# Own semaphores for the weight loads of a mixture-of-experts layer, and two of the loads emitted later

## The chip, the cores and the metric

The kernel runs on the 8 NeuronCores of one Trainium2 chip. The cores do not exchange data: each computes one of the 8 sequences of the batch. What counts is the device time of the slowest core, in microseconds (us).

Each core has a matrix engine (TensorE, PE in the profile; PEld are its weight loads), a vector engine (VectorE, DVE), an activation engine (ScalarE, ACT), a general one (GpSimd, POOL) and SyncE (SP). Each runs its own stream of instructions in order, and they wait for one another on semaphores. DMAs are issued from SyncE's and GpSimd's streams here. Line numbers such as L868 are those of the kernel before.

## The reference

A transformer layer with layer norm ahead of each part. Cut to the second part, in which the change lies:

```python
x = x + attention(layernorm(x))
# flat: [T, D] of layernorm(x); T = 2048 tokens per core, D = 1024, H = 2048, E = 8, top 2
router_probs = softmax(flat @ router_w + router_b)
weights = top-2 of router_probs, zero elsewhere                    # [T, E]
shared_out = gelu(flat @ sw1 + sb1) @ sw2 + sb2
h1 = gelu(einsum('td,edh->teh', flat, rw1) + rb1)                  # all 8 experts, all tokens
expert_out = einsum('teh,ehd->ted', h1, rw2) + rb2
x = x + shared_out + einsum('ted,te->td', expert_out, weights)
```

## The kernel before

The program is written as a plan: `P.emit(engine, fn, waits, inc)` appends one instruction to the list of an engine, with the semaphores and counts that it waits for and the semaphore that it raises. Five semaphores exist: ST, SV and SS, raised by TensorE, VectorE and ScalarE, SQ by the DMAs of SyncE and GQ by the DMAs of GpSimd. `emit` treats the last two in a special way:

```python
        waits = tuple((s, self.cnt[s] if s in ("SQ", "GQ") else v)
                      for (s, v) in waits)
```

A wait for SQ or GQ is thus turned into a wait for all DMAs of that queue that were emitted so far, whichever count was given.

The stages of a core, one behind the other: layer norm and attention with its output projection (to about 1714 us of the profile), second layer norm and router (to about 1846 us), nine experts (to about 4245 us: expert 0 is the shared one, 1 to 8 the routed ones, each over all 2048 tokens), and the store of XRES.

The activations are kept transposed, features on the partitions: XLN (bf16) is the normalised input, XRES (float32) the running result. An expert has W1 (1024 x 2048) and W2 (2048 x 1024), each 4 MB as bf16 in one buffer of its own; the float32 source is cast by the DMA. `emit_mm1(e, tt)` computes a token tile of 512: for each of 16 blocks of hidden features 8 matmuls into one of four slots of PM1 (L729), then a Gelu with the bias B1C by ScalarE into H1G (L746), and for the routed experts a product with WB, the routing weights broadcast to all partitions, by VectorE (L795). `emit_mm2(e, tt)` does for each of 8 output blocks 16 matmuls from H1G and W2 (L817) and one for the bias row B2S (L827) into PM2, and VectorE adds the result to XRES (L834). H1G has two halves, so the order of an expert is mm1(0), mm1(1), mm2(0), mm1(2), mm2(1), mm1(3), mm2(2), mm2(3).

At the head of each routed expert (L843 to L883) five DMAs are emitted on GpSimd, in the order W1 (L845; waits for the last mm1 of the expert before), WROW (L848; one row of routing weights), B1C (L853), B2S (L858) and W2 (L863; the last two wait for the last mm2 of the expert before). Behind them the broadcast is emitted: four times a matmul of ONES with a quarter of WROW into a slot of PM1 (L868) and a copy into WB by VectorE (L877). L868 waits for GQ, for its slot, and for the counts of ScalarE and VectorE as they stand at that point of the plan. Then comes emit_mm1(e, 0).

`barrier()` makes all engines wait for all semaphores; it stands behind the first layer norm, behind attention and ahead of the store.

Of the kernel before, what the change touches and what calls it, by code (L numbers as in the profile page):

```python
# [14 lines left out]
D = 1024  # L15
# [53 lines left out]
def build_program():  # L69
    nc = bass.Bass("TRN2", target_bir_lowering=False)  # L70
# [10 lines left out]
    w2cat = dt("w2cat", [NEXP, 128, (DFF // 128) * D], F32, kind="ExternalInput").ap()  # L81
    b1col = dt("b1col", [NEXP, 128, 16], F32, kind="ExternalInput").ap()
    b2row = dt("b2row", [NEXP, 1, D], F32, kind="ExternalInput").ap()
# [8 lines left out]
    with ExitStack() as ctx:  # L92
        E = ctx.enter_context
# [3 lines left out]
            "SS": E(nc.semaphore("SS")),  # L97
            "SQ": E(nc.semaphore("SQ")),
            "GQ": E(nc.semaphore("GQ")),
        }  # L100
        P = Plan(sems)
        C = P.cnt
# [18 lines left out]
        def barrier():  # L121
            for eng in ("tensor", "vector", "scalar"):
                assert P.tail_inc[eng], f"barrier: {eng} tail lacks inc"
            w = [(k, C[k]) for k in ("ST", "SV", "SS", "SQ", "GQ")]
            for eng in ENGS:
                P.emit(eng, lambda e: e.nop(), waits=w, neutral=True)

        sq_x = []
        for c in range(NCH):
# [3 lines left out]
                inc="SQ", inc_n=16))  # L133
        sq_ones = P.emit("sync", lambda e: e.dma_start(out=ONES[:], in_=c_ones),
                         inc="SQ", inc_n=16)
# [111 lines left out]
        try:  # L247
# [6 lines left out]
            with ExitStack() as actx:  # L254
# [54 lines left out]
                for h in range(min(H, DBG["nheads"])):  # L309
# [32 lines left out]
                    for mt in (range(NMT) if DBG["qkv_parts"] in ("all", "v") else []):  # L342
# [10 lines left out]
                               waits=w)  # L353
# [159 lines left out]
            with ExitStack() as fctx:  # L513
# [12 lines left out]
                gq_rbr = P.emit("gpsimd", lambda e: e.dma_start(out=RBR[:], in_=rwb_row),  # L526
                                inc="GQ", inc_n=16)
                gq_w1 = [P.emit("gpsimd", lambda e: e.dma_start(out=W1[:], in_=w1cat[0]),
                                inc="GQ", inc_n=16)]
                gq_w2 = [P.emit("gpsimd", lambda e: e.dma_start(out=W2[:], in_=w2cat[0]),  # L530
                                inc="GQ", inc_n=16)]
                gq_b1 = [P.emit("gpsimd",
                                lambda e: e.dma_start(out=B1C[:, 0:16], in_=b1col[0]),
                                inc="GQ", inc_n=16)]
                gq_b2 = [P.emit("gpsimd",
                                lambda e: e.dma_start(out=B2S[0:1, 0:D], in_=b2row[0]),
                                inc="GQ", inc_n=16)]

                ln2_done = emit_ln([[] for _ in range(NCH)])
                _ckpt("ln2")  # L540
# [171 lines left out]
                def emit_mm1(e_i, tt, wb_ready, mm1_first_w):  # L712
                    buf = tt % 2
                    last_marker = None
                    for ht in range(16):
# [20 lines left out]
                            if r is not None:  # L736
                                tmm = r
                        h1sl = H1G[:, buf * 8192 + ht * 512: buf * 8192 + (ht + 1) * 512]
                        gw = [("ST", tmm), ("GQ", gq_b1[e_i])]
                        if ht == 0:  # L740
                            gw.append(h1g_free[buf])
                        if e_i == 0 and tt == 0 and ht == 0:
# [58 lines left out]
                def emit_mm2(e_i, tt, h1_ready):  # L801
                    buf = tt % 2
                    last_st = 0
                    for dtl in range(NCH):
                        slot = state["rot2"] % 4
                        state["rot2"] += 1
                        psv = PM2[:, slot * 512:(slot + 1) * 512]
                        for kc in range(16):
                            w = []
                            if kc == 0:  # L810
                                w = [pm2_free[slot], h1_ready]
                                if len(vx_hist) >= 2:
                                    w.append(("SV", vx_hist[-2]))
                                if dtl == 0 and tt == 0:
                                    w.append(("GQ", gq_w2[e_i]))
                            P.emit("tensor",
                                   lambda e, psv=psv, kc=kc, dtl=dtl, buf=buf: e.matmul(  # L817
                                       psv,
                                       W2[:, kc * D + dtl * 128: kc * D + (dtl + 1) * 128],
                                       H1G[:, buf * 8192 + kc * 512:  # L820
                                           buf * 8192 + (kc + 1) * 512],
                                       start=(kc == 0), stop=False),
                                   waits=w)
                        rhs = (WB[0:1, tt * 512:(tt + 1) * 512] if e_i > 0
                               else ONES[0:1, 0:512])
                        tr = P.emit("tensor",
                               lambda e, psv=psv, dtl=dtl, e_i=e_i, rhs=rhs: e.matmul(  # L827
                                   psv,
                                   B2S[0:1, dtl * 128:(dtl + 1) * 128],
                                   rhs, start=False, stop=True),  # L830
                               waits=[("GQ", gq_b2[e_i])], inc="ST")
                        last_st = tr
                        vx = P.emit("vector",
                               lambda e, psv=psv, dtl=dtl, tt=tt: e.tensor_add(  # L834
                                   xres(dtl)[:, tt * 512:(tt + 1) * 512],
                                   xres(dtl)[:, tt * 512:(tt + 1) * 512], psv),
                               waits=[("ST", tr)], inc="SV")
                        pm2_free[slot] = ("SV", vx)
                        state["xadd"] = vx
                    return ("ST", last_st)  # L840

                for e_i in range(min(NEXP, DBG["nexp"])):
                    if e_i > 0:  # L843
                        gq_w1.append(P.emit("gpsimd",
                                lambda e, e_i=e_i: e.dma_start(out=W1[:], in_=w1cat[e_i]),  # L845
                                waits=[w1_free], inc="GQ", inc_n=16))
                        gq_wrow = P.emit("gpsimd",
                                lambda e, e_i=e_i: e.dma_start(  # L848
                                    out=WROW[:], in_=WSB[e_i - 1:e_i, :]),
                                waits=[("SV", router_done_sv), wrow_free],  # L850
                                inc="GQ", inc_n=16)
                        gq_b1.append(P.emit("gpsimd",
                                lambda e, e_i=e_i: e.dma_start(  # L853
                                    out=B1C[:, (e_i % 2) * 16:(e_i % 2) * 16 + 16],
                                    in_=b1col[e_i]),
                                waits=[b1_free[e_i % 2]], inc="GQ", inc_n=16))
                        gq_b2.append(P.emit("gpsimd",
                                lambda e, e_i=e_i: e.dma_start(  # L858
                                    out=B2S[0:1, 0:D],
                                    in_=b2row[e_i]),  # L860
                                waits=[b2_free], inc="GQ", inc_n=16))
                        gq_w2.append(P.emit("gpsimd",
                                lambda e, e_i=e_i: e.dma_start(out=W2[:], in_=w2cat[e_i]),  # L863
                                waits=[w2_free], inc="GQ", inc_n=16))
                        wb_evac = 0
                        for r in range(4):
                            tb_ = P.emit("tensor",
                                    lambda e, r=r: e.matmul(  # L868
                                        PM1[:, r * 512:(r + 1) * 512],
                                        ONES[0:1, 0:128],  # L870
                                        WROW[0:1, r * 512:(r + 1) * 512],
                                        start=True, stop=True),
                                    waits=[("GQ", gq_wrow), pm1_free[r],
                                           ("SS", C["SS"]), ("SV", C["SV"])],
                                    inc="ST")
                            wb_evac = P.emit("vector",
                                    lambda e, r=r: e.tensor_copy(  # L877
                                        WB[:, r * 512:(r + 1) * 512],
                                        PM1[:, r * 512:(r + 1) * 512]),
                                    waits=[("ST", tb_), wb_free], inc="SV")  # L880
                            pm1_free[r] = ("SV", wb_evac)
                        wrow_free = ("ST", tb_)
                        wb_ready = ("SV", wb_evac)  # L883
                    else:
                        wb_ready = ("SV", 0)

                    mm1_first_w = [("GQ", gq_w1[e_i])]
                    if e_i == 0:
                        mm1_first_w += [("SV", ln2_done),
                                        ("SV", router_done_sv),  # L890
# [2 lines left out]

                    h1_ready = {}
                    h1_ready[0] = emit_mm1(e_i, 0, wb_ready, mm1_first_w)
                    if DBG["stop"] == "mm1" and e_i == 0:
                        h1_ready[1] = emit_mm1(e_i, 1, wb_ready, mm1_first_w)
                        _DBGREF["H1G"] = H1G
                        _ckpt("mm1")
# [193 lines left out]
```

How the kernel before makes its waits and increments, by code:

```python
        def run(e, _w=waits, _f=fn, _i=inc, _n=inc_n):  # L57
            for s, v in _w:
                e.wait_ge(sems[s], v)
            inst = _f(e)
            if _i is not None:
                inst.then_inc(sems[_i], _n)
```

## Time and profile before

| | us |
|---|---|
| median of 2 runs | 4270.73 (4269.18 to 4272.28) |
| the profiled execution | 4269.49 |
| its span on the slowest core, core 2 | 4267.8 |
| spans of the eight cores | 4252.6 to 4267.8 |
| busy in the span: PE / DVE / ACT / POOL | 3033.0 / 963.4 / 855.6 / 28.5 |

All numbers of the trace below are of this one profiled execution. The span runs from the first to the last instruction of a core; the execution takes a little longer. "Idle before" in the groups is the time that the engine stood still right ahead of instructions of the group, with the event that ended most of it; for a wait on several semaphores that is the one that came last by the profile. PEclk is the clock that was granted to TensorE, as a share of 2.4 GHz.

### The profile page before, as it was taken

What the parts mean: (1) busy time and instruction counts of PE and PEld (TensorE: products, weight loads), DVE (VectorE), ACT (ScalarE), POOL (GpSimd) and SP (SyncE); (2) the same over time, 40 slices, a digit from 0 to 9 for tenths busy, and PEclk for the clock granted to TensorE, in tenths of its full rate; (3) what the DMA queues carried; (4) which work ended last, traced back from release to release, by engine and by line L of the source; (5) the groups of instructions that cost most, each with busy time, mean ns of one, the idle gap of its engine ahead of it and who ended that gap; (6) DMA issues with size and microseconds to landing.
All of it is one profiled execution on the core that took longest, in us unless ns stands there. A gap on an engine that the chain in (4) does not pass through costs nothing.

```text
span 4267.8 us, 45453 instructions; the slowest of 8 cores (4252.6 to 4267.8 us)
## 1 busy us (share of the span) xinstructions
PE 3033.0 (71%) x15473; PEld 1346.9 (32%) x15668; DVE 963.4 (23%) x2098; ACT 855.6 (20%) x1354; POOL 28.5 (1%) x55
## 2 busy tenths in 40 slices
PE   2455445554555557379699696996969969799797
PEld 0122222222222223134244342443424424344343
DVE  5222222222222222610121121211212212122121
ACT  0223232323222231022021210212102111021110
POOL 0000000000000000000000000000000000000000
PEclk7555555555555557689899898998989989899899
DMA  2100000000000000400402204022040220402201
GB/s 80 30 1 1 1 1 1 1 1 1 1 1 1 1 1 1 80 1 6 74 1 40 40 1 79 1 40 40 1 79 1 40 40 1 79 1 40 40 1 79
DMA packets 7082, 98.76 MB, mean 23 GB/s; under 512 B 1860, under 2 KB 2260, under 8 KB 2260
## 3 DMA queue, kind: packets, MB, share of 16 engines
q0 software_dynamic: 3984, 77.79, 10.1%
q1 hardware_dynamic: 2884, 18.06, 1.2%
q8 instruction: 142, 2.33, 0.2%
q14 instruction: 72, 0.59, 0.0%
HBM read 165.10 MB, written 8.39 MB: 41 GB/s over the span
## 4 chain that ended last, share of the span: by engine, by line
PE 63%; DVE 11%; DMA 10%; issue 8%; ACT 7%; DVEq 1%; ACTq 0%; POOL 0%; SPq 0%; POOLq 0%
PE PM L729 24%; PE PM L817 20%; PE PS L424 5%; DMA W<-w2cat 5%; DVE SMASK L404 4%; ACT PT L409 4%; PE PS L385 4%; ACT PT L395 3%; DMA W<-w1cat 2%; PE PM L827 2%; DMA B1C<-b1col 2%; DVE AVN L441 2%; PE PTR L448 2%; PE PS L330 1%; PE PS L491 1%
## 5 line engine op out<-in xcount | busy, mean ns | idle before, releaser
L817 PE MATMUL PM<-H1G,W 128*128 128x512 bf16 x4518 | 1031.6, 379 | 9.5 <-issue 6.2
L729 PE MATMUL PM<-XLN,W 128*128 128x512 bf16 x4509 | 1009.4, 384 | 8.5 <-issue 2.7
L746 ACT ACTIVATE H1G<-PM,B1C 128x512 bf16<-128x512 f32 x576 | 395.7, 687 | 1935.9 <-PE PM L729 1935.9
L729 PEld LDWEIGHTS PM<-XLN,W 128*128 128x128 bf16 x4608 | 453.3, 99 | 559.9 <-issue 33.6
L817 PEld LDWEIGHTS PM<-H1G,W 128*128 128x128 bf16 x4608 | 429.3, 98 | 541.4 <-issue 59.1
L834 DVE TENSOR_TENSOR XRES<-XRES,PM 128x512 f32<-128x512 f32 x288 | 198.0, 688 | 1014.5 <-PE PM L827 1014.5
L424 PE MATMUL PS<-VA,PT 128*128 128x65 bf16 x2560 | 176.2, 242 | 349.5 <-ACT PT L409 349.5
L795 DVE TENSOR_TENSOR H1G<-H1G,WB 128x512 bf16<-128x512 bf16 x512 | 217.9, 426 | 699.7 <-ACT H1G L746 699.7
L385 PE MATMUL PS<-QT,KT 64*128 64x512 bf16 x640 | 322.4, 600 | 73.2 <-ACT PT L395 72.4
L395 ACT ACTIVATE PT<-PS 128x512 bf16<-128x512 f32 x384 | 209.0, 595 | 566.2 <-PE PS L385 565.7
L448 PE MATMUL PTR<-IDB,AVN 128*64 128x128 bf16 x256 | 68.6, 268 | 321.0 <-DVE AVN L441 321.0
L404 DVE TENSOR_TENSOR SMASK<-PS,MASKS 128x512 f32<-128x512 f32 x256 | 176.9, 691 | 458.6 <-PE PS L385 285.8
L424 PEld LDWEIGHTS PS<-VA,PT 128*128 128x128 bf16 x2560 | 152.3, 131 | 405.7 <-issue 405.7
L409 ACT ACTIVATE PT<-SMASK 128x512 bf16<-128x512 f32 x256 | 161.1, 629 | 325.4 <-DVE SMASK L404 325.4
L868 PE MATMUL PM<-WROW,ONES 1*128 1x512 bf16 x32 | 18.6, 581 | 249.6 <-DMA W<-w2cat 225.3
L385 PEld LDWEIGHTS PS<-QT,KT 64*128 64x128 bf16 x640 | 66.8, 107 | 278.8 <-issue 256.1
L448 PEld LDWEIGHTS PTR<-IDB,AVN 128*64 128x64 bf16 x256 | 31.2, 122 | 356.3 <-issue 356.3
L424 PE MATMUL PS<-VA,ONES 128*128 128x65 bf16 x1536 | 119.0, 242 | 0.0
L436 DVE RECIPROCAL RZ<-PS 128x1 f32<-128x1 f32 x256 | 41.3, 161 | 311.4 <-PE PS L424 308.2
L330 PE MATMUL PS<-XLN,WQ 64*64 64x512 bf16 x128 | 62.7, 616 | 63.5 <-DMA BRR<-br_row 62.3
L460 DVE COPY AVT<-PTR 64x128 bf16<-64x128 bf16 x256 | 56.8, 222 | 190.0 <-PE PTR L448 190.0
L827 PE MATMUL PM<-WB,B2S 1*128 1x512 bf16 x256 | 98.6, 385 | 0.0
(99 smaller groups left out, 928.0 us busy)
## 6 DMA issues: line engine op xcount, KB each, us to landing
W<-w1cat POOLq DMA_DIRECT2D x9, 4096.0 KB, 26.2
W<-w2cat POOLq DMA_DIRECT2D x9, 4096.0 KB, 27.0
XRES<-xt SPq DMA_DIRECT2D x8, 1024.0 KB
ot<-XRES SPq DMA_DIRECT2D x8, 1024.0 KB
WRF<-wr_rl POOLq DMA_DIRECT2D x1, 2048.0 KB, 18.8
MASKS<-c_masks SPq DMA_DIRECT2D x1, 1024.0 KB
B1C<-b1col POOLq DMA_DIRECT2D x9, 8.0 KB, 26.4
B2S<-b2row POOLq DMA_DIRECT2D x9, 2.0 KB, 3.2
```

The lines of the kernel that those rows point to most:

```text
L385: lambda e, psv=psv, kc=kc, j=j: e.matmul(psv, KT[0:64, kc * 128:(kc + 1) * 128], QT[0:64, j * 512:(j + 1) * 512], start=True, stop=True),
L395: lambda e, pts=pts, psv=psv: e.activation(pts, psv, AF.Exp, scale=0.125),
L404: lambda e, smsl=smsl, psv=psv, d=d: e.tensor_mul(smsl, psv, MASKS[:, d * 512:(d + 1) * 512]),
L409: lambda e, pts=pts, smsl=smsl: e.activation(pts, smsl, AF.Exp, scale=0.125),
L424: lambda e, lhs=lhs, mt=mt, kc=kc: e.matmul(PS1[:, mt * 65:(mt + 1) * 65], lhs, VA[:, kc * 65:(kc + 1) * 65], start=(mt == 0 and kc == 0), ...
L448: lambda e, mt=mt, off=off: e.transpose(PTR[off:off + 64, (mt % 2) * 128:(mt % 2) * 128 + 128], AVN[:, mt * 64:(mt + 1) * 64], IDB[:], til ...
L729: lambda e, psv=psv, kc=kc, ht=ht, tt=tt: e.matmul(psv, W1[:, kc * DFF + ht * 128: kc * DFF + (ht + 1) * 128], xln(kc)[:, tt * 512:(tt + 1 ...
L746: lambda e, h1sl=h1sl, psv=psv, e_i=e_i, ht=ht: e.activation(h1sl, psv, AF.Gelu, bias=B1C[:, (e_i % 2) * 16 + ht: (e_i % 2) * 16 + ht + 1]),
L795: lambda e, h1sl=h1sl, tt=tt: e.tensor_mul(h1sl, h1sl, WB[:, tt * 512:(tt + 1) * 512]),
L817: lambda e, psv=psv, kc=kc, dtl=dtl, buf=buf: e.matmul(psv, W2[:, kc * D + dtl * 128: kc * D + (dtl + 1) * 128], H1G[:, buf * 8192 + kc * 512:
L827: lambda e, psv=psv, dtl=dtl, e_i=e_i, rhs=rhs: e.matmul(psv, B2S[0:1, dtl * 128:(dtl + 1) * 128], rhs, start=False, stop=True),
L834: lambda e, psv=psv, dtl=dtl, tt=tt: e.tensor_add(xres(dtl)[:, tt * 512:(tt + 1) * 512], xres(dtl)[:, tt * 512:(tt + 1) * 512], psv),
```

## The change

Five semaphores are added, for the loads of W1, W2, WROW, B1C and B2S, and each of these loads raises its own instead of GQ. Who reads such a buffer waits for its semaphore. Since `emit` rewrites only the counts of SQ and GQ, a wait for one of the new ones keeps the count that is given, that is, the one load meant. The loads of B2S and W2 of the routed experts are emitted behind emit_mm1(e, 0) instead of ahead of the broadcast. `barrier()` waits for all ten semaphores (where their count is above zero).

```diff
+            "W1S": E(nc.semaphore("W1S")),
+            "W2S": E(nc.semaphore("W2S")),
+            "WRS": E(nc.semaphore("WRS")),
+            "B1S": E(nc.semaphore("B1S")),
+            "B2S_": E(nc.semaphore("B2S_")),
...
-            w = [(k, C[k]) for k in ("ST", "SV", "SS", "SQ", "GQ")]
+            w = [(k, C[k]) for k in C]
...
-                        gw = [("ST", tmm), ("GQ", gq_b1[e_i])]
+                        gw = [("ST", tmm), ("B1S", gq_b1[e_i])]
...
                                 if dtl == 0 and tt == 0:
-                                    w.append(("GQ", gq_w2[e_i]))
+                                    w.append(("W2S", gq_w2[e_i]))
...
-                               waits=[("GQ", gq_b2[e_i])], inc="ST")
+                               waits=[("B2S_", gq_b2[e_i])], inc="ST")
...
                         gq_w1.append(P.emit("gpsimd",
                                 lambda e, e_i=e_i: e.dma_start(out=W1[:], in_=w1cat[e_i]),
-                                waits=[w1_free], inc="GQ", inc_n=16))
+                                waits=[w1_free], inc="W1S", inc_n=16))
...
                                 waits=[("SV", router_done_sv), wrow_free],
-                                inc="GQ", inc_n=16)
+                                inc="WRS", inc_n=16)
...
-                                waits=[b1_free[e_i % 2]], inc="GQ", inc_n=16))
-                        gq_b2.append(P.emit("gpsimd",
-                                lambda e, e_i=e_i: e.dma_start(
-                                    out=B2S[0:1, 0:D],
-                                    in_=b2row[e_i]),
-                                waits=[b2_free], inc="GQ", inc_n=16))
-                        gq_w2.append(P.emit("gpsimd",
-                                lambda e, e_i=e_i: e.dma_start(out=W2[:], in_=w2cat[e_i]),
-                                waits=[w2_free], inc="GQ", inc_n=16))
+                                waits=[b1_free[e_i % 2]], inc="B1S", inc_n=16))
                         wb_evac = 0
                         for r in range(4):
...
-                                    waits=[("GQ", gq_wrow), pm1_free[r],
+                                    waits=[("WRS", gq_wrow), pm1_free[r],
                                            ("SS", C["SS"]), ("SV", C["SV"])],
...
-                    mm1_first_w = [("GQ", gq_w1[e_i])]
+                    mm1_first_w = [("W1S", gq_w1[e_i])]
...
                     h1_ready[0] = emit_mm1(e_i, 0, wb_ready, mm1_first_w)
+                    if e_i > 0:
+                        gq_b2.append(P.emit("gpsimd",
+                                lambda e, e_i=e_i: e.dma_start(
+                                    out=B2S[0:1, 0:D],
+                                    in_=b2row[e_i]),
+                                waits=[b2_free], inc="B2S_", inc_n=16))
+                        gq_w2.append(P.emit("gpsimd",
+                                lambda e, e_i=e_i: e.dma_start(out=W2[:], in_=w2cat[e_i]),
+                                waits=[w2_free], inc="W2S", inc_n=16))
```

The loads of expert 0 (emitted ahead of the second layer norm) change their semaphores in the same way.

## Rows read from the trace of the kernel before

**Rows 1.** Spans of three cores, with the mean granted clock

```profile
core 0: 4252.6 us, clock 0.780
...
core 2: 4267.8 us, clock 0.780
...
core 7: 4262.6 us, clock 0.781
```

**Rows 2.** The page's groups: busy, mean ns of one, idle before, releaser

```profile
L817 PE MATMUL PM<-H1G,W 128*128 128x512 bf16 x4518 | 1031.6, 379 | 9.5 <-issue 6.2
...
L868 PE MATMUL PM<-WROW,ONES 1*128 1x512 bf16 x32 | 18.6, 581 | 249.6 <-DMA W<-w2cat 225.3
```

**Rows 3.** List of waits, core 2, then core 7: us in total, times, longest

```profile
PE PM L868 <- DMA W<-w2cat: 225.3, 8, 29.2
...
PE PM L868 <- DMA W<-w2cat: 217.5, 8, 27.6
```

**Rows 4.** Timeline, core 2, from expert 0 to 1: start, us, engine, line

```profile
2079.61 3.63 PE L817 MATMUL PM<-H1G,W 128*128 128x512 bf16 x16
...
2083.16 0.39 PE L827 MATMUL PM<-ONES,B2S 1*128 1x512 bf16 x1
2083.66 0.69 DVE L834 TENSOR_TENSOR XRES<-XRES,PM 128x512 f32<-128x512 f32 x1 [3.19 <-PE PM L827]
...
2084.60 0.56 POOL L863 DMA_DIRECT2D W<-w2cat  x1
...
2112.71 0.58 PE L868 MATMUL PM<-WROW,ONES 1*128 1x512 bf16 x1 [29.16 <-DMA W<-w2cat]
2113.46 0.69 DVE L877 CAST WB<-PM 128x512 bf16<-128x512 f32 x1 [29.11 <-PE PM L868]
...
2114.30 0.58 PE L868 MATMUL PM<-WROW,ONES 1*128 1x512 bf16 x1 [1.01 <-DVE WB L877]
...
2118.40 16.92 PE L729 MATMUL PM<-XLN,W 128*128 128x512 bf16 x70 [0.34 <-issue]
```

**Rows 5.** Issue to landing: W2 (L863), all loads into W, WROW, in this order

```profile
DMA to landing us min/median/max: 25.0/26.8/27.6
...
DMA to landing us min/median/max: 24.7/26.7/51.7
...
DMA to landing us min/median/max: 24.3/25.6/26.6
```

**Rows 6.** The chain that ended last, core 2, in order of time: start, us, what

```profile
2118.40 12.17 PE PM L729 x49
2130.63 10.74 PE PM L729 x49
...
2175.04 3.45 PE PM L817 x16
...
2388.71 11.85 PE PM L729 x49
...
2658.84 13.30 PE PM L729 x49
```

**Rows 7.** Windows, core 2: length, busy by engine, PEclk, DMA share, GB/s

```profile
1806.00:1808.00 2.00, 0.99 (x5) 0.52 (x5) 0.50 (x3) 0.00 (x0) 0.00 (x0) 0.82 0.00 0
...
2087.00:2088.00 1.00, 0.00 (x0) 0.00 (x0) 0.00 (x0) 0.00 (x0) 0.00 (x0) 0.58 3.20 524
...
2130.00:2354.00 224.00, 222.42 (x989) 95.73 (x1007) 46.44 (x90) 40.53 (x59) 1.59 (x3) 1.00 0.11 20
```

**Rows 8.** Timeline, core 2, at other places

```profile
1717.48 1.43 POOL L530 DMA_DIRECT2D W<-w2cat  x1
1717.57 1.22 DVE L164 CAST XLN<-XRES 128x2048 bf16<-128x2048 f32 x1
...
2022.72 0.50 POOL L848 DMA_DIRECT2D WROW<-WSB  x1
...
2040.84 3.63 PE L817 MATMUL PM<-H1G,W 128*128 128x512 bf16 x16
```

More of the change, by code:

```diff
@@ L528, in build_program @@
                 gq_w1 = [P.emit("gpsimd", lambda e: e.dma_start(out=W1[:], in_=w1cat[0]),
-                                inc="GQ", inc_n=16)]
+                                inc="W1S", inc_n=16)]
                 gq_w2 = [P.emit("gpsimd", lambda e: e.dma_start(out=W2[:], in_=w2cat[0]),
-                                inc="GQ", inc_n=16)]
+                                inc="W2S", inc_n=16)]
                 gq_b1 = [P.emit("gpsimd",
                                 lambda e: e.dma_start(out=B1C[:, 0:16], in_=b1col[0]),
-                                inc="GQ", inc_n=16)]
+                                inc="B1S", inc_n=16)]
                 gq_b2 = [P.emit("gpsimd",
                                 lambda e: e.dma_start(out=B2S[0:1, 0:D], in_=b2row[0]),
-                                inc="GQ", inc_n=16)]
+                                inc="B2S_", inc_n=16)]
                 ln2_done = emit_ln([[] for _ in range(NCH)])
```

## Prediction

> **What bounds the kernel now.** I began with the spans of the cores [rows 1]: all eight compute the same program on their own sequence, core 2 is the slowest at 4267.8 us, and core 0, the shortest, is only 15 us below it, so what happens alike on all cores decides. The page's table of groups [rows 2] then says where TensorE works: L817, the second matmul of the experts, has 4,518 matmuls and is busy for 1031.6 us, and L729, the first, is its like. The line to stop at is a small one. L868, the broadcast of an expert's routing weights, has 32 matmuls and 18.6 us of work, but 249.6 us of idle time lies before them, and 225.3 us of that is put down to the DMA that fills W from w2cat.
>
> The list of waits gives this core by core [rows 3]: 8 such waits, one for each routed expert, 225.3 us in total and 29.2 us at most on core 2, 217.5 us on core 7.
>
> The timeline around the first change of expert [rows 4] shows the order. The last matmul of expert 0 (L827) starts at 2083.16 and takes 0.39 us, so it ends at 2083.55. VectorE adds it to XRES until 2083.66 + 0.69 = 2084.35. GpSimd, released by the last second-stage matmul, issues B2S and then, at 2084.60, W2. Then nothing computes until the first L868 at 2112.71. Four rounds of L868 and a VectorE copy (L877) follow, 1.59 us apart (2112.71 to 2114.30), and L729 starts at 2118.40. From 2084.60 to 2112.71 are 28.1 us, and the transfer of W2 takes 25.0 to 27.6 us [rows 5]. The period of an expert is 2388.71 - 2118.40 = 270.3 us [rows 6]; 28 us of it is this hole.
>
> Is it a real need? L868 reads WROW and ONES only. WROW was issued at 2022.72 and lands after 24.3 to 26.6 us [rows 5, 8], by 2050, while TensorE is still in the second matmul of the expert before. What holds L868 is the form of the wait: the count of GQ that is written into it is the count of all DMAs emitted so far, and W2 and B2S are emitted ahead of it. Nothing in L868, L877 or the first L729 reads W2. On the path that sets the end the wait can be taken away without anything else having to be faster.
>
> **The change, part by part.**
>
> *The wait of L868.* With WRS it asks for WROW alone. It keeps its other waits: PM1's slot, and the counts of ScalarE and VectorE at that point. The latter is the last L834, ended at 2084.35. From the end of a VectorE instruction to the matmul that it releases takes 0.15 us (L877 of 2113.46 + 0.69 = 2114.15, then L868 at 2114.30 [rows 4]). So L868 starts at 2084.50, 0.95 us behind the last matmul rather than 29.16 us. Of each wait about 0.95 us stays, 8 x 0.95 = 7.6 us of the total. Core 2 gains 225.3 - 7.6 = 217.7 us and comes to 4267.8 - 217.7 = 4050.1 us. Core 7 waited less and gains 217.5 - 7.6 = 209.9 us: 4262.6 - 209.9 = 4052.7 us. The same sum on the other cores stays below core 7, so after the change core 7 is the last by this reckoning, and the program gains 4267.8 - 4052.7 = 215.1 us, not 217.7.
>
> *The four rounds.* They stay chained to one another, since the count of VectorE in each takes in the copy before: 2118.40 - 2112.71 = 5.69 us from the first L868 to the first L729. I keep this at its full price. It could be shorter: at 1.2 GHz a one-row matmul takes 0.58 us (L868), at 2.4 GHz 0.39 us (L827) [rows 4], so 4 x 0.19 = 0.8 us for each expert, 6 us in all, if the clock is up.
>
> *The clock.* Behind the hole TensorE runs at the half level, 1.2 GHz, for a while. The first 49 matmuls of an expert take 11.85 to 13.30 us (at 2388.71 and 2658.84, the smallest and the largest of eight) against 10.74 us in full run [rows 6]; the eight average 12.56, so the ramp costs 1.8 us each, 14.5 us in all. Does it go away with the hole? In the hole the granted clock is 0.58 over 2087 to 2088: it fell then, some 4 us behind the last full matmul [rows 7]. After the change there will be 2083.55 to 2090.19, 6.6 us, with only four short matmuls in it. The router stage has the nearest pattern: its bursts of L575 bring the clock to 1.00 and a few small transposes later it is down again, 0.82 over 1806 to 1808 where it passes from one to the other [rows 7]. So I take the clock to fall again at each change of expert, and the ramp to cost what it costs now: no gain. The ends: 14.5 us gained if it never falls; if each ramp is like the worst of today, 13.30 - 12.56 = 0.74 us more, 6 us lost in all.
>
> *W2 and B2S move behind the first emit_mm1.* On GpSimd's queue their order does not change (W1, WROW, B1C, B2S, W2), nor what each waits for, so W2 is still issued at 2084.60 and nothing new is queued behind a wait. What changes is who needs it: the first L817 of the expert. It comes at 2175.04, 56.6 us behind the first L729 [rows 6]; after the change at 2090.2 + 56.6 = 2146.8. W2 would have to take 2146.8 - 2084.6 = 62.2 us to be late. Its transfers take 25.0 to 27.6 us, and the slowest weight load of the run, with two issued back to back, 51.7 us [rows 5]. Both ends are hidden: cost nothing, cover 34 us over the usual, 10 us over the worst. B2S is issued before W2 and needed after it. If the cover were gone, W2 would be late by its excess over 62.2 us, eight times.
>
> *W2's transfer now runs beside matmuls.* That costs nothing if TensorE doesn't feel it. W1's transfer does so already: 16 matmuls of L817 take 3.63 us at 2040.84, in the middle of W1's load (issued just ahead of WROW at 2022.72), and 3.63 us at 2079.61 without one [rows 4, 8]. New beside it are ScalarE's L746 and VectorE's L795, which TensorE has to wait for only after two tiles.
>
> *Descriptors.* The issue of W2 took 0.56 us at a change of expert, and 1.43 us at 1717.48, where VectorE was casting XLN (L164) at the same time [rows 4, 8]; that load was also the 51.7 us one. After the change L877's copies and L795 run beside W2's issue. The Trainium skill (SBUF — State Buffer, on the "DVE blocks DMA" trap) says that a VectorE instruction in a two-port mode, as such a cast can be, keeps GpSimd from writing the descriptors of its DMAs. The long issue at 1717.48 fits this. By rule or by row the load stays under the 62.2 us above, and the sum is the same unless it is far slower than any seen; this is a rival below.
>
> *First expert, router, barriers.* The waits of expert 0 and of the router now name fewer DMAs. They don't bind: the loads are issued at 1717 and last 51.7 us at most, to 1769, and the router is still at work at 1806 [rows 5, 7]. The last barrier gets five more waits on each engine, all met. L868 gets through its four waits and starts within the 0.15 us above; so five more, met long before, cost 0 to 0.3 us; I take 0.3.
>
> **The sum.** The profiled execution took 4269.49 us, 1.7 us more than its span. 4052.7 + 1.7 + 0.3 = 4054.7 us against that. The median of the two runs, 4270.73 us, lies 1.2 us above the profiled execution, so 4055.9, say 4056 us: 5.0% less.
>
> **The rivals.**
>
> *The clock stays up between experts.* The 6.6 us are not empty, and the clock falls late. For it: it took about 4 us to fall with nothing at all running. Against it: the router's rows. It gives 6 + 14.5 = 20.5 us more: 4035 us. Chance 0.12.
>
> *The dense run pulls the clock down (the other side).* TensorE now rests 28 us in each 270, on all eight cores nearly at once. Without the rest there are nine stretches of about 235.5 us (the period less the 34.85 us from 2083.55 to 2118.40), 2120 us, almost back to back. If a share f of them ran at 1.2 GHz rather than 2.4, that would cost up to f x 2120 us, and from f = 0.10 on the change would lose. With f = 0.2 it costs 424 us: 4480 us. Against it: within a stretch there is no sign of it; 2130 to 2354 show a granted clock of 1.00 and 222 of 224 us busy [rows 7], and the mean clock of cores on either die is the same to 0.001 [rows 1]. If tens of microseconds of load brought it, these would show it. For it: only that no stretch before was longer than these. The Trainium skill (TensorE: Matmul & The Clock Gate, on the peak-current limiter) says that once three cores of a die run dense matmuls the whole die goes to 13/16 of its clock within 5 to 20 us. By that page the 2120 us would become 2609, and the sum about 4545 us. The trace of before disagrees, with 1.00 long after 20 us while all eight cores compute. Chance 0.05.
>
> *W2 comes late after all.* Descriptors written beside VectorE, or banks shared with busy engines, make a 27 us load three times as long, 80 us: 18 us late, eight times, 143 us, so 4199 us. It starts at 62.2 us. Against it: the worst load of the run and W1's loads beside matmuls. Chance 0.02.
>
> *The hole has a second owner.* L868 still waits for something that comes with W2, so that the wait stays under another name, 4270 us. Against it: WROW and VectorE's last add are both done by 2084.35, and PM1's slots were free soon after the last L729, which W1's load at 2022 had waited for. Chance 0.03.
>
> **How the numbers follow.** My forecast, 4056 us, has 0.78. Its own range, from ramps (6 us worse) and from which core comes last (all within 5 us), is 4043 to 4068. The range that I give also takes in the clock that stays up and leaves out the late W2, the dragging clock and the second owner, 0.10 together: 4030 to 4075. The measurement of this kernel can tell about 2% (85 us) from no change. Faster by more than that: 0.78 + 0.12 = 0.90. Within 2%: late W2 and second owner, 0.05. Slower: 0.05.
>
> **What would show it.** Right: the 8 waits of L868 for W2 are gone, what idle time is left before the first of four is about 1 us and owned by L834; L868's first start lies about 1 us behind L827's end; the period of an expert is near 243 us; W2 still lands 25 to 28 us after its issue, and no L817 waits for it. The granted clock is 0.50 for a few microseconds at each change of expert, and the first 49 matmuls stay at 12 to 13 us. Wrong: 10.8 us for them (clock up), a granted clock under 1.00 in the middle of a stretch (load), L817 waiting for a DMA (late W2), or L868 waiting for a DMA (second owner).

## The result and the profile after

| | before | after |
|---|---|---|
| median, us | 4270.04 | 4051.93 |
| ratio, 95% interval | | 0.9509 (0.9479 to 0.9539) |
| slowest core of the profiled execution, us | 4267.8 | 4051.3 (second profile, below) |

By the medians the kernel is 5.1% faster (4051.93 / 4270.04 = 0.949); 4056 us, 5.0% less, was predicted, 4030 to 4075 as the range. In some executions of either kernel a few cores run for a stretch at a lower granted clock, and the times below are of executions without that unless said. The ratio in the table is one of means and takes in two that have such stretches (4104.66 and 4076.87 us), so it lies above the ratio of the medians.

The first profiled execution after the change holds such stretches on four cores, so I profiled the changed kernel a second time, beside experiment e6, and read the change from that trace. Its cores:

```profile
core 0: 4044.6 us, clock 0.798
core 1: 4049.8 us, clock 0.793
core 2: 4047.2 us, clock 0.797
...
core 6: 4051.3 us, clock 0.794
core 7: 4046.4 us, clock 0.795
```

The lines have moved: L729 of before is L734 now, L817 is L822, L827 is L832, L834 is L839, the broadcast L868 and its copy L877 are L865 and L874, the load of W2 is L900. The list of waits of the second profile, core 6 (us in total, times, longest), has two entries for the broadcast where [rows 3] has the one of 225.3 us:

```profile
PE PM L865 <- DVE WB L874: 24.3, 24, 1.0
PE PM L865 <- DVE XRES L839: 7.5, 8, 0.9
```

Eight waits of 0.94 us are left, owned by the addition to XRES (L839), as the prediction's step said. The timeline of the same core from expert 0 to 1, which answers to [rows 4]:

```profile
2085.99 0.39 PE L832 MATMUL PM<-ONES,B2S 1*128 1x512 bf16 x1
2086.48 0.69 DVE L839 TENSOR_TENSOR XRES<-XRES,PM 128x512 f32<-128x512 f32 x1 [3.19 <-PE PM L832]
...
2087.32 0.37 PE L865 MATMUL PM<-WROW,ONES 1*128 1x512 bf16 x1 [0.94 <-DVE XRES L839]
2087.43 0.56 POOL L900 DMA_DIRECT2D W<-w2cat  x1
...
2088.70 0.37 PE L865 MATMUL PM<-WROW,ONES 1*128 1x512 bf16 x1 [1.01 <-DVE WB L874]
...
2090.09 0.58 PE L865 MATMUL PM<-WROW,ONES 1*128 1x512 bf16 x1 [1.01 <-DVE WB L874]
...
2091.68 0.58 PE L865 MATMUL PM<-WROW,ONES 1*128 1x512 bf16 x1 [1.01 <-DVE WB L874]
...
2092.59 3.62 PE L734 MATMUL PM<-XLN,W 128*128 128x512 bf16 x8 [0.33 <-issue]
```

The broadcast now starts 0.94 us behind the last matmul of the expert, and W2's load is issued within it, at 2087.43, as before right after the last second-stage matmul. The first two rounds run at the full clock (0.37 us a matmul), the last two at half of it (0.58 us): the clock falls in the hole that is left. Its windows (length, busy by engine, then the granted clock, DMA share, GB/s):

```profile
2088.00:2090.00 2.00, 0.37 (x1) 0.09 (x1) 1.25 (x2) 0.00 (x0) 0.00 (x0) 0.99 0.32 50
2090.00:2092.00 2.00, 0.90 (x2) 0.20 (x2) 0.69 (x1) 0.00 (x0) 0.00 (x0) 0.50 1.28 213
```

The chain that ended last, core 6, shows the ramp behind it (the matmuls that still run at the lower clock) and the new period, the answer to [rows 6]:

```profile
2092.59 12.82 PE PM L734 x49
2105.46 10.74 PE PM L734 x49
...
2335.29 12.64 PE PM L734 x49
```

From 2092.59 to 2335.29 are 242.7 us, against 270.3 before; the broadcasts of all experts put the mean at 242.4 us (the first group's last at 2091.68, the eighth's at 3788.8, seven periods). W2 takes 26.7 to 28.1 us from issue to landing on this core. The first L822 of the expert starts at 2149.87 in the same chain, 57.3 us behind the first L734 and 62.4 us behind W2's issue, and no L822 waits for a DMA.

### The profile page after: what moved, and what is told of

It is laid out like the page before. It is cut to its first block, busy times and chain, and to the rows that moved or that the text cites. A ratio compares the mean times of both kernels' runs of the same rounds, so it can differ in the third digit from the quotient of the medians.

```text
span 4102.8 us, 45478 instructions; the slowest of 8 cores (4046.5 to 4102.8 us)
## 1 busy us (share of the span) xinstructions
PE 3085.2 (75%) x15473; PEld 1358.9 (33%) x15668; DVE 963.5 (23%) x2098; ACT 855.7 (21%) x1354; POOL 28.5 (1%) x55
## 4 chain that ended last, share of the span: by engine, by line
PE 71%; DVE 12%; issue 8%; ACT 7%; DMA 1%; DVEq 1%; ACTq 0%; SPq 0%; POOL 0%
PE PM L734 25%; PE PM L822 25%; PE PS L429 6%; DVE SMASK L409 4%; ACT PT L414 4%; PE PS L390 4%; ACT PT L400 3%; PE PM L832 2%; DVE AVN L446 2%; PE PTR L453 2%; PE PS L335 2%; PE PS L496 1%; DVE RZ L441 1%; PE PS L351 1%; PE PS L360 1%
## 5 line engine op out<-in xcount | busy, mean ns | idle before, releaser
L822 PE MATMUL PM<-H1G,W 128*128 128x512 bf16 x4518 | 1053.2, 385 | 9.8 <-issue 7.1
L734 PE MATMUL PM<-XLN,W 128*128 128x512 bf16 x4509 | 1041.7, 392 | 9.1 <-issue 2.7
L734 PEld LDWEIGHTS PM<-XLN,W 128*128 128x128 bf16 x4608 | 460.9, 100 | 584.9 <-issue 141.7
L822 PEld LDWEIGHTS PM<-H1G,W 128*128 128x128 bf16 x4608 | 433.9, 99 | 557.6 <-issue 124.8
L839 DVE TENSOR_TENSOR XRES<-XRES,PM 128x512 f32<-128x512 f32 x288 | 198.2, 688 | 1037.5 <-PE PM L832 1037.5
L832 PE MATMUL PM<-WB,B2S 1*128 1x512 bf16 x256 | 99.9, 390 | 0.0
L429 PEld LDWEIGHTS PS<-VA,ONES 128*128 128x128 bf16 x1536 | 97.9, 132 | 0.0
## 6 DMA issues: line engine op xcount, KB each, us to landing
W<-w1cat POOLq DMA_DIRECT2D x9, 4096.0 KB, 28.6
```

Source lines behind the costliest of these rows:

```text
L429: lambda e, lhs=lhs, mt=mt, kc=kc: e.matmul(PS1[:, mt * 65:(mt + 1) * 65], lhs, VA[:, kc * 65:(kc + 1) * 65], start=(mt == 0 and kc == 0), ...
L734: lambda e, psv=psv, kc=kc, ht=ht, tt=tt: e.matmul(psv, W1[:, kc * DFF + ht * 128: kc * DFF + (ht + 1) * 128], xln(kc)[:, tt * 512:(tt + 1 ...
L822: lambda e, psv=psv, kc=kc, dtl=dtl, buf=buf: e.matmul(psv, W2[:, kc * D + dtl * 128: kc * D + (dtl + 1) * 128], H1G[:, buf * 8192 + kc * 512:
L832: lambda e, psv=psv, dtl=dtl, e_i=e_i, rhs=rhs: e.matmul(psv, B2S[0:1, dtl * 128:(dtl + 1) * 128], rhs, start=False, stop=True),
L839: lambda e, psv=psv, dtl=dtl, tt=tt: e.tensor_add(xres(dtl)[:, tt * 512:(tt + 1) * 512], xres(dtl)[:, tt * 512:(tt + 1) * 512], psv),
```

## The experiments

All are cut from the changed kernel or from the one before. Not tried: the move of the two loads without new semaphores. By the rule in `emit` it too would leave the broadcast with the counts of W1, WROW and B1C only, as e9 does, so it may well give the same gain; that is argued and not shown. Against using it: a count that several loads in flight raise does not say which of them has landed. So that half of the change is judged only by leaving it out.

**e1, the semaphores without the move.** B2S and W2 are emitted ahead of the broadcast again:

```diff
+                        gq_b2.append(P.emit("gpsimd",
...
+                        gq_w2.append(P.emit("gpsimd",
...
                         wb_evac = 0
                         for r in range(4):
...
                     h1_ready[0] = emit_mm1(e_i, 0, wb_ready, mm1_first_w)
-                    if e_i > 0:
-                        gq_b2.append(P.emit("gpsimd",
...
-                        gq_w2.append(P.emit("gpsimd",
```

> The five semaphores alone, with B2S and W2 emitted where they stood before (ahead of the broadcast). My theory: what counts is the count that L868 waits for, and the order on GpSimd's queue is the same with the move and without, so this gives the time of the changed kernel, 4052 us (4047 to 4057). Rival (the move of the two loads is what frees TensorE): without it the wait is back, 4270 us, or some part of the way.

Measured: 4052.6 and 4052.8 us, and the same two waits of 0.94 and 1.0 us. The instructions on every engine's list, their order and their waits are those of the changed kernel, since no other instruction of GpSimd's stands between the old place of the two loads and the new. The move does nothing once the loads have semaphores of their own.

**e9, two semaphores instead of five.** The kernel before, with only W2 and B2S on their own semaphores and nothing moved:

```diff
-                                waits=[b2_free], inc="GQ", inc_n=16))
+                                waits=[b2_free], inc="B2S_", inc_n=16))
...
-                                waits=[w2_free], inc="GQ", inc_n=16))
+                                waits=[w2_free], inc="W2S", inc_n=16))
```

(and the same for expert 0 and the two readers)

> The kernel before with only W2 and B2S on semaphores of their own; W1, WROW and B1C stay on GQ, no load is moved. My theory: the wait of L868 for all of GQ then means W1, WROW and B1C, landed 30 us earlier, so this is worth the whole change: 4052 us (4047 to 4057). Rival (waits for W1 or B1C that the shared count held up had their part, too): the time stays above 4060 us.

Measured: 4052.56 us in one execution of four. In the three others (4104, 4106 and 4219 us) only cores 0 and 1 are longer, at a lower mean clock; the spans of cores 2 to 7 are 4043.2 to 4051.5 us, like the changed kernel's. The profile, which is one of these three, names VectorE alone as the owner of the broadcast's waits, on core 4:

```profile
PE PM L870 <- DVE WB L879: 24.3, 24, 1.0
PE PM L870 <- DVE XRES L836: 7.5, 8, 0.9
```

So W1S, WRS and B1S are worth nothing that can be measured; the whole gain is that the broadcast no longer counts the loads of W2 and B2S. Which of the two matters is shown by e3.

**e3, the one wait put back.** As e1, and

```diff
-                                    waits=[("WRS", gq_wrow), pm1_free[r],
+                                    waits=[("WRS", gq_wrow), ("W2S", gq_w2[e_i]), pm1_free[r],
```

> As the kernel with the semaphores alone, but the broadcast waits for W2's semaphore too: the one wait put back, all else of the change kept. My theory: 8 x 27.2 us come back and nothing else, 4268 us (4263 to 4275), with 8 waits of the broadcast's matmul for W2 of 27 to 29 us. Rival (part of the gain is from the other split waits, on B1C, B2S and W1, or from the clock): it stays below 4255 us. For the clock: with 28 us of rest at each expert no stretch at a granted clock of 0.81 appears.

Measured: 4269.9 and 4271.8 us, the time of before to 0.1%, and the old entry is back in the list of waits (core 0):

```profile
PE PM L873 <- DMA W<-w2cat: 229.7, 8, 30.6
```

The wait is the sole owner of the difference. The part of the expectation on the clock did not hold: in two of the four executions cores had a lower mean clock (4568 and 4673 us); the last section takes it up.

**e4 and e5, how much cover W2 has.** W2 of each routed expert is loaded twice (e4) or three times (e5), one load behind the other, and the second stage waits for the last:

```diff
-                        gq_w2.append(P.emit("gpsimd",
-                                lambda e, e_i=e_i: e.dma_start(out=W2[:], in_=w2cat[e_i]),
-                                waits=[w2_free], inc="W2S", inc_n=16))
+                        w2w = w2_free
+                        for _n in range(2):
+                            gw2 = P.emit("gpsimd",
+                                lambda e, e_i=e_i: e.dma_start(out=W2[:], in_=w2cat[e_i]),
+                                waits=[w2w], inc="W2S", inc_n=16)
+                            w2w = ("W2S", gw2)
+                        gq_w2.append(gw2)
```

(three in e5)

> The changed kernel with each routed expert's W2 loaded twice, the second load after the first has landed, and the second matmul waits for the second: the transfer that must be hidden is twice as long. The prediction put the point from which W2 is late at 62.2 us after its issue. One load took 28.1 to 29.7 us in the changed kernel, so two take 57 to 61 us: still hidden, 4052 us (4047 to 4060), L822 without a wait for a DMA. Rival (the load slows TensorE down, or is already at its edge): 4060 us and more, growing with the bytes moved.

Measured for e4: in each of the four executions some cores are longer at a lower mean clock; the shortest took 4107 and 4108 us, and in the profiled one these are cores 0 and 1 alone. Its six other cores have spans of 4045.8 to 4051.2 us, like the changed kernel's, and on none of them does an L822 wait for a DMA. By these cores twice the transfer is hidden.

> The same with three loads in a row: 3 x 28.8 us and two more issues of 0.6 to 2 us, 87 to 90 us after the first issue against the 62.2 us (about 61 with the shorter broadcast of the changed kernel), so 26 us late at each of eight experts: 4052 + 8 x 26 = 4260 us (4235 to 4280), and the wait shows at the first matmul of the second stage. Rival (slack was larger than reckoned, or transfers run faster while TensorE waits): under 4200 us. If it is right together with the run of two loads, the point lies between 58 and 88 us and the size of the miss gives it.

Measured for e5: 4207 and 4213 us, outside my 4235 to 4280. The timeline of core 4, expert 1, and the row of its waits tell why:

```profile
2083.85 0.56 POOL L902 DMA_DIRECT2D W<-w2cat  x1
2113.74 0.53 POOL L902 DMA_DIRECT2D W<-w2cat  x1 [29.33 <-DMA W<-w2cat]
2143.27 0.53 POOL L902 DMA_DIRECT2D W<-w2cat  x1 [28.99 <-DMA W<-w2cat]
...
2170.32 5.97 PE L822 MATMUL PM<-H1G,W 128*128 128x512 bf16 x16 [24.03 <-DMA W<-w2cat]
```

```profile
PE PM L822 <- DMA W<-w2cat: 139.4, 8, 24.0
```

L822 starts at 2170.32 after 24.03 us of waiting, so it was ready at 2146.3, 62.4 us behind the first issue. The point from which W2 is late, put at 62.2 us, holds. What I missed was the transfer: I took the 28.8 us of the first profile, and here a load lands 26.1 us after its issue in the median, so the eight waits average 17.4 us and not 26. The waits explain 139 us of the 155 to 161 that this kernel is slower than the changed one. The rest is a second fall of the clock: it is 0.50 when L822 starts again (window 2170 to 2174), and the first 16 L822 behind the eight stalls take 5.11 to 6.38 us, where 16 take 3.56 in full run, 17 us in all. Together with e4 the two runs put the point between two loads and three, and the wait itself gives it to a few tenths.

**e8, the four rounds without their chain.** The broadcast's matmuls wait for WROW and their slot only:

```diff
-                                    waits=[("WRS", gq_wrow), pm1_free[r],
-                                           ("SS", C["SS"]), ("SV", C["SV"])],
+                                    waits=[("WRS", gq_wrow), pm1_free[r]],
```

> The changed kernel, but the four broadcast matmuls wait for WROW and for their slot of PM1 only, no longer for all that VectorE and ScalarE had done by then. They can then follow the last matmul of the expert before at 0.23 us each, and the first L734 waits for the first copy into WB only (about 1.6 us behind L832's end: the last L839 of 0.69, the copy of 0.69, 0.15 to 0.2 us of hand-over). In the changed kernel about 6 us pass. This tells the price of the chain from that of the clock: if the clock then stays at 1.00 across the change, the ramp of some 2 us goes too, 8 x (4.4 + 2) = 51 us: 4001 us (3995 to 4010). If it falls all the same, 8 x 4.4 = 35 us: 4017 us.

Measured: 4013.8 and 4013.7 us, between my two cases (the ratio, 0.9418 with 0.932 to 0.9516, also takes in an execution of 4066.5 us). Timeline and windows of core 3:

```profile
2084.59 0.39 PE L832 MATMUL PM<-ONES,B2S 1*128 1x512 bf16 x1
2084.81 1.02 PE L865 MATMUL PM<-WROW,ONES 1*128 1x512 bf16 x4
2086.95 5.34 PE L734 MATMUL PM<-XLN,W 128*128 128x512 bf16 x24 [1.11 <-DVE WB L873]
```

```profile
2086.00:2088.00 2.00, 1.05 (x5) 0.52 (x6) 2.00 (x4) 0.00 (x0) 0.58 (x2) 1.00 0.00 0
2088.00:2092.00 4.00, 4.00 (x20) 1.85 (x19) 1.21 (x3) 1.37 (x2) 0.00 (x0) 1.00 1.39 230
...
2322.00:2324.00 2.00, 0.89 (x5) 0.25 (x4) 1.90 (x4) 0.00 (x0) 1.05 (x2) 1.00 0.00 0
2324.00:2328.00 4.00, 4.00 (x12) 1.44 (x11) 1.27 (x3) 0.69 (x1) 0.00 (x0) 0.57 0.89 140
```

From the end of L832 to the first L734 are 1.97 us, 3.8 us less than in the changed kernel on a core without gaps in its records (core 7: 2081.21 to 2087.01, 5.8 us): 8 x 3.8 = 31 us. The other 7 us are the clock. At the change to expert 1 it stays at 1.00; at the next, with the same hole, it is 0.57 over 2324 to 2328, and 12 matmuls run where 20 did. The first 256 L734 of an expert take 55.41 us at three of the eight changes of core 3 and 57.10 at five, against 57.27 to 57.62 at all eight of e1 and 55.36 in e6, where nothing falls: 16 us of ramps before, 9 us here. My two cases took it to be one or the other; it is both, by turns.

**e6, the broadcast under the second stage.** WB has two halves. WROW of the next expert is loaded early, into a row of WSB's tensor (there was no room for both otherwise), and the four broadcast matmuls stand one each behind the output blocks 1 to 4 of the last emit_mm2:

```diff
+                        if bcast_for is not None and 1 <= dtl <= 4:
+                            state["tb"], state["wbev"] = emit_bcast(bcast_for, dtl - 1)
...
-                                    waits=[("WRS", gq_wrow), pm1_free[r],
-                                           ("SS", C["SS"]), ("SV", C["SV"])],
+                    w = [("WRS", gq_wrow[e_n]), pm1_free[r]]
...
-                    h1g_free[1] = emit_mm2(e_i, 3, h1_ready[3])
+                    h1g_free[1] = emit_mm2(e_i, 3, h1_ready[3],
+                                           e_i + 1 if e_i + 1 < NEXP else None)
```

> The changed kernel with two buffers for WB, and the four broadcast matmuls of the next expert set between the output blocks of the last emit_mm2 of the expert before, without the waits on one another; WROW is loaded early, into a free row of WSB's tensor. What is left of the hole at a change of expert (about 6.0 us from the last matmul to the first of the next expert in the changed kernel) goes, less four matmuls of 0.23 us, and with it the fall of the clock. Period now 242.4 us on core 0, of which 233.7 us are dense work: 8.7 us of overhead, 7.8 us of it to win, 8 x 7.8 = 62 us: 3990 us (3980 to 4000), and a granted clock of 1.00 across the change. If the clock fell although the hole is gone, only 8 x 5.1 = 41 us: 4011 us. For the stretches at 0.81 of the clock: if uninterrupted matmul work brings them, they are more frequent here than in the changed kernel, where 4 of 13 executions had them; if they are independent of it, as frequent.

Measured: 3988.99 us in the median, 3988.3 to 3989.4 in five executions, ratio to before 0.9342 (0.9329 to 0.9354). It beats both kernels: 1.6% less than the changed one. Timeline and window of core 5 across the change of expert:

```profile
2081.58 3.63 PE L843 MATMUL PM<-H1G,W 128*128 128x512 bf16 x16
2085.14 0.39 PE L854 MATMUL PM<-ONES,B2S 1*128 1x512 bf16 x1
2085.45 9.89 PE L734 MATMUL PM<-XLN,W 128*128 128x512 bf16 x45
```

```profile
2086.00:2090.00 4.00, 4.00 (x21) 1.75 (x19) 0.74 (x2) 1.37 (x2) 1.54 (x3) 1.00 0.78 132
```

No hole, and no fall of the clock. That confirms the size of what the changed kernel still pays at each expert: 62 us in eight, predicted from its period, 63 measured. It also goes against the fear that matmuls without a rest must pull the clock down: 2.1 ms without a gap, and five executions within 1.1 us.

**e7, the changed kernel again**, on the same chip:

> The changed kernel itself, beside the kernel without the last hole on the same chip: 4052 us in undisturbed executions. For the stretches at 0.81 of the clock: about one execution in three with some core pair 27 us longer per stretch (4077, 4104 and so on) if they come from dense work without rests, none in the kernel before beside it.

Measured: 4052.37 us in the median; ratio 0.9489 (0.9476 to 0.9502). The part of the expectation on the clock fell: one of five executions of this kernel had cores with a lower mean clock (4182 us), and so had one of the nine of the kernel before beside it (4658 us).

## Why the prediction was right

*The wait and its owner.* Right, and shown by e3 (put back alone, it brings back 4270 us) and e9 (the waits for W2 and B2S taken out alone, they give the whole gain). The second owner (0.03) is excluded.

*What is left of it.* 0.95 us forecast, 0.94 measured, 7.5 us in all against 7.6.

*Which core comes last.* The span of the slowest core was forecast at 4052.7 us and is 4051.3. That it would be core 7 was wrong: core 7 has 4046.4 us, 6.3 less than my sum for it, and core 6 is last, for which the same sum (4267.3 - 227.3 + 7.6) gave 4047.6, 3.7 too little. That the two maxima agree to 1.4 us is therefore in part luck; the sum is good to some 6 us on a single core. The cores now lie within 7 us, and the waits on which I sorted them have no part in it: from the first broadcast to the eighth every core takes 1701.4 or 1701.5 us, and what differs is when the first one starts (2087.3 us on core 6, 2082.1 on core 7), ahead of the routed experts.

*The rounds.* Kept at full price, 0 to 6 us named as the bound. Two of the four run at the full clock, so the rounds are some 0.4 us shorter for each expert, 5.69 us before and 5.27 us now (2087.32 to 2092.59): 3.4 us in all, which the forecast left out.

*The clock.* Right: it falls again within the 6 us hole (0.50 over 2090 to 2092), and the first 49 matmuls of the expert take 12.82 and 12.64 us, inside the 11.85 to 13.30 of [rows 6]; the eight of core 6 average 12.56 us, as before. The rival in which it stays up (0.12) is excluded for this hole; e8 and e6 show what it takes: with a hole of 2 us the clock stayed up at three changes of eight, and without a hole it did not fall. The router's rows [rows 7] were the right neighbour to read.

*W2 beside matmuls.* Right. The cover was put at 62.2 us, and e5 measured 62.4. W2 lands a little later than before: 25.3 to 28.6 us after its issue in the second profile, as medians of the eight cores, against 25.1 to 26.9, and far from the cover. The Trainium skill's rule on VectorE and GpSimd's descriptors (SBUF — State Buffer, the "DVE blocks DMA" trap), named in the prediction, was hardly put to a test: W2's issue takes 0.56 us (2087.43 to 2087.99), as it did with VectorE idle [rows 4], but L874's first copy begins only at 2087.86 and reads PM, not a buffer in SBUF as the cast at 1717 did.

*The load on the clock (the other side, 0.05).* It did not decide the time: in the second profile the clock is 0.99 over 2094 to 2320, and e6 shows that dense work of 2.1 ms can go without any fall. But the sign that the prediction named for it, a clock under 1.00 in the middle of a stretch, is there on four cores of the first profile. The last section tells what is known of it.

*The device time.* Forecast 4056, measured 4052: 1.4 us of the difference lie in the span and 0.3 in what I had added for the barrier, since the second profiled execution took 4053.0 us, again 1.7 more than its span, and not 4054.7. The other 2.3 us are scatter between executions: the median lies 1.1 us below that execution, and I had put it 1.2 above.

## What to carry to other kernels

Where several loads share a semaphore and the count of a wait is rewritten to "all so far", each reader waits for the slowest load counted, and the source hides that; look in the profile for a small operation with a long wait owned by a transfer that it does not read. Two semaphores, for the big late load and the one ahead of it, were enough. Once such a hole is closed, look at what is left of it: 6 us of chained handovers cost another 2 us here each time in clock ramp, and spreading them under dense work won back all of it, 63 us.

## What the runs showed of the hardware

In the first profile of the changed kernel the granted clock has a third value. Windows of 160 us, on core 2, then core 0 (same die), then core 4 (the other die) later on; the last three numbers are the granted clock, the DMA share and GB/s:

```profile
3550.00:3710.00 160.00, 158.94 (x588) 63.36 (x599) 28.95 (x60) 30.93 (x45) 0.00 (x0) 0.81 0.08 14
...
3550.00:3710.00 160.00, 160.00 (x728) 69.59 (x726) 34.81 (x72) 39.16 (x57) 0.00 (x0) 1.00 0.10 17
...
3795.00:3955.00 160.00, 158.94 (x588) 63.42 (x599) 28.78 (x59) 30.91 (x45) 0.00 (x0) 0.81 0.08 14
```

At 0.81 a core does 588 matmuls where, with the same missing records, it does 714 at 1.00 (core 4, 3550 to 3710), so one such stretch costs 27 to 29 us: core 2 had two and has a span of 4102.8 us, core 4 had one and has 4076.9, core 0 none and has 4048.0. Cores 2 and 3 had them together, and so had 4 and 5, while their neighbours on the die computed at 1.00. The Trainium skill (TensorE: Matmul & The Clock Gate, the peak-current limiter) gives this value, 13/16, for a whole die under dense work of three cores or more, held while the load lasts. The value agrees; the rest differs here: pairs of cores rather than a die, an end at about 3711 us with the load unchanged (0.97 over 3715 to 3815), and no core longer than the rest in 8 of the 13 executions of the changed kernel and in the ten of the kernel before beside them. I had expected such stretches to come from work without rests. The runs do not settle that. Outside the traces one can only count the executions in which some cores are longer at a lower mean clock. On two chips they were about as frequent with the rests of 28 us (the kernel before and e3) as without: 7 executions of 11 beside 6 of 8 of e1 and e4, and 1 of 9 beside 1 of 10 of e6 and e7. Beside e8 and e9 they were 2 of 7 with the rests and 5 of 8 without, and in the measurement of the result none of 10 and 5 of 13 (the expectation of e6 says 4). That e6 had none in five executions says little on a chip where 2 of 19 had them. So work without rests need not bring them, and as far as mean clocks tell they come without it too; whether it makes them more frequent, and what sets them off, stays open.
